# Values projected first, row parts among the first scores, in a fused decoder layer on one core

## The reference, cut to what matters

```python
# x: (2, 256, 512)   ctx: (2, 512, 512)
x = layernorm(x + self_attention(x))      # 32 heads of 16, causal, ALiBi bias, w_attn 512x1536, w_proj 512x512
x = layernorm(x + cross_attention(x, ctx))# 32 query heads, 8 key/value heads of 128, keys from [ctx; x], rms-normed q and k
x = layernorm(x + ffn(x))                 # block-diagonal, permuted
# self_attention:
qkv = x @ w_attn + b_attn; q, k, v = split(qkv, 3)
scores = where(causal, q @ k.T / 16 + slope * (j - i), -inf)
out = softmax(scores) @ v @ w_proj + b_proj
# cross_attention (keys and values):
kv = concat([ctx, x]); k = rms_norm(kv @ Wk) * k_norm; v = kv @ Wv
```

## Time and profile before

| | us |
|---|---|
| median of 3 runs | 844.86 (843.57 to 845.25) |
| profiled execution | 844.77, its span 843.0 |
| PE busy in the span | 826.2 (98%) |
| DVE, ACT, POOL busy | 547.3, 475.4, 522.6 |
| granted clock of TensorE | 0.999 of full |

### The profile page before, as it was taken

The page is one execution under the profiler, slowest core; times in us unless marked ns, Lnnn a source line. Parts: engine busy times, 40 slices in busy tenths (PEclk is TensorE's granted clock), DMA queues, the critical chain, the costliest instruction groups (busy, mean ns, idle before and its releaser), DMA issues.

```text
span 843.0 us, 15129 instructions
## 1 busy us (share of the span) xinstructions
PE 826.2 (98%) x4851; PEld 694.1 (82%) x4851; DVE 547.3 (65%) x1507; ACT 475.4 (56%) x1006; POOL 522.6 (62%) x676
## 2 busy tenths in 40 slices
PE   7999999999999999999999999999999999999997
PEld 5777777777788888888888888888888888888874
DVE  4456566766355677667767676667766766777664
ACT  4666665666246655455555555555545555556554
POOL 3477876757426476766666755775676566636931
PEclk9999999999999999999999999999999999999999
DMA  6613223222141721112102111121122100100101
GB/s 197 199 54 113 75 77 114 63 66 62 51 138 51 243 74 52 50 58 69 51 19 76 34 64 68 37 68 68 37 61 75 38 2 19 63 1 1 26 1 51
DMA packets 48510, 56.22 MB, mean 67 GB/s; under 512 B 4670, under 2 KB 29772, under 8 KB 48460
## 3 DMA queue, kind: packets, MB, share of 16 engines
q1 hardware_dynamic: 48460, 55.59, 21.0%
HBM read 41.95 MB, written 13.63 MB: 66 GB/s over the span
## 4 chain that ended last, share of the span: by engine, by line
PE 62%; DVE 2%; ACT 2%; issue 0%; POOL 0%; POOLq 0%
PE bank L1537 15%; PE bank L48 11%; PE bank L50 11%; PE bank L49 11%; PE bank L1594 9%; PE bank L1527 1%; ACT prob L1351 1%; DVE x_mx L1422 1%; ACT prob L1742 1%; PE bank L1867 0%; PE bank L1868 0%; DVE pT_lo L1471 0%; PE bank L1899 0%; PE bank L1909 0%; PE bank L1908 0%
## 5 line engine op out<-in xcount | busy, mean ns | idle before, releaser
L1253 POOL TENSOR_SCALAR prob<-prob,x_rinv 128x768 f32<-128x768 f32 x124 | 112.9, 911 | 166.8 <-DVE x_rinv L1431 166.8
L1368 ACT ACTIVATE pT_hi<-bank 128x512 fp32r<-128x512 f32 x192 | 114.4, 598 | 90.2 <-PE bank L1594 89.2
L1351 ACT ACTIVATE prob<-bank,x_nm,q_rms 128x768 f32<-128x768 f32 x124 | 123.3, 994 | 47.2 <-DVE x_nm L1425 46.8
L1471 DVE TENSOR_TENSOR pT_lo<-bank,pT_hi 128x512 fp32r<-128x512 f32 x192 | 130.3, 679 | 5.4 <-ACT pT_hi L1368 4.0
L1422 DVE TENSOR_REDUCE x_mx<-bank 128x1 f32<-128x768 f32 x124 | 118.2, 953 | 21.9 <-PE bank L1537 21.6
L1594 PE MATMUL bank<-ident,prob 128*128 128x128 f32 x768 | 115.0, 272 | 2.1 <-POOL prob L1253 1.3
L1594 PEld LDWEIGHTS bank<-ident,prob 128*128 128x128 f32 x768 | 95.0, 140 | 14.2 <-POOL prob L1253 2.0
L48 PE MATMUL bank<-pT_hi,xv_hi 128*128 128x512 f32 x192 | 86.5, 451 | 0.4 <-DVE pT_lo L1471 0.2
L485 ACT ACTIVATE s_self<-s_self,nm_self 128x128 f32<-128x128 f32 (+1 forms) x128 | 57.1, 448 | 43.0 <-DVE nm_self L628 42.4
L50 PE MATMUL bank<-pT_hi,xv_lo 128*128 128x512 f32 x192 | 75.7, 394 | 0.0
L49 PE MATMUL bank<-pT_lo,xv_hi 128*128 128x512 f32 x192 | 75.4, 393 | 0.0
(11 more groups left out here) (234 smaller groups left out, 2048.2 us busy)
## 6 DMA issues: line engine op xcount, KB each, us to landing
wo_raw<-in_Wo SPq DMA_DIRECT2D x8, 1024.0 KB, 5.1
v_by_head<-v_st SPq DMA_DIRECT2D x12, 512.0 KB, 3.6
kT_by_head<-kT_st SPq DMA_DIRECT2D x12, 512.0 KB, 3.2
xk_raw<-kT_by_head SPq DMA_DIRECT2D x16, 384.0 KB, 3.1
xv_raw<-v_by_head SPq DMA_DIRECT2D x16, 384.0 KB, 3.2
wq_raw<-in_Wq SPq DMA_DIRECT2D x6, 1024.0 KB, 5.5
wq_raw<-in_w_attn SPq DMA_DIRECT2D x12, 256.0 KB, 4.1
xk_raw<-in_ctx SPq DMA_DIRECT2D x8, 256.0 KB, 2.6
```

The lines of the kernel that those rows point to most:

```text
L1253: nc.gpsimd.tensor_scalar(prob[:, s, :], prob[:, s, :], rinv[:, s:s + 1], 1.0, ALU.mult, ALU.mult)\
L1351: nc.scalar.activation(prob[:, s, :].rearrange("p (a e) -> p a e", a=2), bank[:, at:at + 2, 0:HALF], ACT.Exp, bias=nm[:, s:s + 1], scale=q ...
L1368: nc.scalar.activation(pT_hi[:, a, :], bank[:, turn.bank[s, what, a], :], ACT.Copy)\
L1471: nc.vector.tensor_tensor(pT_lo[:, a, :], bank[:, turn.bank[s, what, a], :], f32(pT_hi[:, a, :]), ALU.subtract).then_inc(ring_out, 1)
```

## The change

The value weights (group 2 of w_attn) become weight group 0, queries and keys groups 1 and 2. x and the value weights are loaded alternately, piece by piece. PE projects values of a row tile as soon as it and a weight piece are split, then queries, then keys; the context's first tile is transposed between queries and keys, into bank 1; the bias columns go through bank 0. The first four parts stand between S(0) and S(1). The low halves of groups 3 and 5 (Wk's first half, Wv's first) move from POOL to DVE; those of group 6 are placed piece by piece. The cycles that begin with S(3), S(5), S(7) and S(8) lose their last part, so from S(9) on the list has the parts where it had them. As CT(0) has left the ring, banks 4 and 7 change roles.

```diff
-    order = [("S", 0), ("W", 5), ("V", 0), ("E", (0, 0)), ("V", 1), ("E", (0, 1)), ("V", 2), ("E", (0, 2)), ("CT", 0), ("CX", 0), ("V", 3),
-             ("E", (0, 3)), ("R", (0, 0)), ("W", 6), ("R", (0, 1))]
+    order = [("S", 0)]
...
+    order += [("WH6", 0), ("WH6", 1), ("WH6", 2)]
+    parts(1)
+    order.append(("E", (0, 0)))
+    parts(1)
+    order += [("E", (0, 1)), ("WL6", 0), ("WL6", 1)]
+    parts(1)
+    order += [("E", (0, 2)), ("E", (0, 3)), ("R", (0, 0)), ("WL6", 2)]
+    parts(1)
+    order += [("R", (0, 1)), ("WH6", 3), ("WL6", 3)]
...
-        if c < NQ - 1:
+        if c not in (2, 4, 6, 7, NQ - 1):
             parts(1)
...
-        ON_VECTOR, ON_POOL = (0, 1, 2, 4, 6, 8), (3, 5, 7)
+        ON_VECTOR, ON_POOL = (0, 1, 2, 3, 4, 5, 6, 8), (7,)
...
-        before = {4: ("V", 0), 7: ("V", 3), 5: ("V", 1), 6: ("V", 2)}
-        place, quad, rows_over = {}, 0, {}
+        before = {4: ("K", 0), 7: ("K", 3), 5: ("K", 1), 6: ("K", 2)}
+        place, quad, rows_over = {("CT", 0): (1, None)}, 0, {}
...
+                    if p == 0:
+                        sp.dma_start(x[:, i, :], d["x"].rearrange("b s d -> (b s) d")[tokens(i), :]).then_inc(x_in[i], 16)
...
+            load_context(0)
             load_weights(2)
-            load_context(0)
...
+            def values(i, j):
+                pe.wait_ge(xt_lo, j + 1)
+                pe.wait_ge(w_los, i + 1)
+                last = three_passes(nc, bank[:, 4 + j, :], xT_hi[:, i, tokens(j)], xT_lo[:, i, tokens(j)],
+                                    w_hi[:, 0, i, :], w_lo[:, 0, i, :], i == 0, i == KT - 1)
+                if i == KT - 1:
+                    last.then_inc(v_ps, 1)
+
+            row_transposes(0)
+            row_transposes(1)
+            values(0, 0)
+            row_transposes(2)
+            for i, j in ((0, 1), (1, 0), (1, 1)):
+                values(i, j)
+            row_transposes(3)
+            for i, j in ((0, 2), (1, 2), (2, 0), (2, 1), (2, 2), (0, 3), (1, 3), (2, 3)):
+                values(i, j)
+            for j in range(TT):
+                values(KT - 1, j)
+            pe.wait_ge(bias_in, 48)
+            nc.tensor.transpose(bank[:, 0, 0:NCOLS], col_rows[:], ident[0:NCOLS, 0:NCOLS]).then_inc(col_ps, 1)
             for m in range(2 * KT):
+                if m == KT:
+                    context_transposes(0)
+                if m < KT:
+                    pe.wait_ge(v_out, 2 * (m + 1))
...
+                else:
+                    pe.wait_ge(col_out, 1)
+                    pe.wait_ge(ct_lo, 1)
```

More of the change, by code:

```diff
@@ L520, in copy_keys, with take_values_of @@
                 nc.scalar.activation(k_sq[:], k_rows[:, w, :], ACT.Square).then_inc(ksq_made, 1)
+            def take_values_of(j):
+                act.wait_ge(v_ps, j + 1)
+                for odds in range(2):
+                    lanes = slice(odds * SA_DIM, (odds + 1) * SA_DIM)
+                    nc.scalar.activation(padded[odds][:, j, :, lanes],
+                                         bank[:, 4 + j, :].rearrange("p (g e) -> p g e", e=2 * SA_DIM)[:, :, lanes],
+                                         ACT.Copy).then_inc(v_out, 1)
             for j in range(TT):
@@ L525, in _, with queries_of @@
                     .then_inc(xt_hi, 1)
[L526 to L529, removed]
+                weights_hi(0, j)
             for i in range(KT):
                 weights_hi(1, i)
+            act.wait_ge(zeros, 2)
+            for j in range(TT):
+                take_values_of(j)
+            act.wait_ge(col_ps, 1)
+            nc.scalar.activation(cols[:], bank[:, 0, 0:NCOLS], ACT.Copy).then_inc(col_out, 1)
             act.wait_ge(col_out, 1)
-            for m in range(KT):
+            def queries_of(m):
                 act.wait_ge(qk_ps, m + 1)
@@ L536, in _, with keys_of @@
                     .then_inc(q_out, 1)
[L537 to L541, removed]
+            def keys_of(m):
                 act.wait_ge(qk_ps, KT + m + 1)
@@ L544, in _ @@
                                      scale=even[:]).then_inc(k_out, 1)
-                weights_hi(4, m)
-            act.wait_ge(zeros, 2)
-            for what, a in ORDER:
[L548 to L555, removed]
+            for i in range(KT):
+                weights_hi(2, i)
+            queries_of(0)
+            queries_of(1)
+            weights_hi(3, 0)
+            weights_hi(3, 1)
+            queries_of(2)
+            weights_hi(3, 2)
+            weights_hi(3, 3)
+            weights_hi(4, 0)
+            queries_of(3)
+            context_hi(0)
+            for i in range(1, KT):
+                weights_hi(4, i)
+            act.wait_ge(nw_made, 2)
+            keys_of(0)
+            weights_hi(5, 0)
+            weights_hi(5, 1)
+            keys_of(1)
+            weights_hi(5, 2)
+            weights_hi(5, 3)
+            keys_of(2)
+            keys_of(3)
+            for what, a in ORDER:
+                if what == "CX":
                     context_hi(a)
@@ L569, in _ @@
                         weights_hi(a, i)
+                elif what == "WH6":
+                    weights_hi(6, a)
                 elif what == "WH":
@@ L676, in _, with odd_keys @@
                                         f32(xT_hi[:, :, tokens(j)]), ALU.subtract).then_inc(xt_lo, 1)
-            for p in range(2):
-                for i in range(KT):
-                    early_lo(p, i)
+                early_lo(0, j)
+            for i in range(KT):
+                early_lo(1, i)
+            def odd_keys(m):
+                dve.wait_ge(qk_ps, KT + m + 1)
+                dve.wait_ge(k_out, m + 1)
+                nc.vector.tensor_scalar(kT_odd[:, m, :], bank[:, 4 + m, :], cols[:, KT + m:KT + m + 1],
+                                        odd[:], ALU.add, ALU.mult).then_inc(k_odd_out, 1)
+            for i in range(KT):
+                early_lo(2, i)
             dve.wait_ge(col_out, 1)
@@ L685, in _ @@
             for i in range(KT):
[L686 to L692, removed]
+                early_lo(3, i)
+            early_lo(4, 0)
+            context_lo(0)
+            for i in range(1, KT):
+                early_lo(4, i)
+            odd_keys(0)
+            early_lo(5, 0)
+            early_lo(5, 1)
+            odd_keys(1)
+            early_lo(5, 2)
+            early_lo(5, 3)
+            odd_keys(2)
+            odd_keys(3)
             for what, a in ORDER:
@@ L696, in _ @@
                         early_lo(a, i)
+                elif what == "WL6":
+                    early_lo(6, a)
                 elif what == "CX":
@@ L796, in drained, with context_transposes, row_transposes @@
                     pe.wait_ge(vg_late, i[0] + 1)
-            pe.wait_ge(const, 4)
-            for j in range(TT):
+            def context_transposes(n):
+                pe.wait_ge(c_in, 16 * (n + 1))
+                if n > 0:
+                    drained("CT", n)
+                for i in range(KT):
+                    last = nc.tensor.transpose(bank[:, bank_of("CT", n), tokens(i)], c_raw[:, tokens(i)], ident[:])
+                last.then_inc(ct_ps, 1)
+            def row_transposes(j):
                 pe.wait_ge(x_in[j], 16)
@@ L815, in _ @@
                     if m % KT == 0:
-                        pe.wait_ge(w_los, m + i + 1)
-                    last = three_passes(nc, bank[:, 4 + m % KT, :], w_hi[:, m // KT, i, w], w_lo[:, m // KT, i, w],
+                        pe.wait_ge(w_los, KT + m + i + 1)
+                    last = three_passes(nc, bank[:, 4 + m % KT, :], w_hi[:, 1 + m // KT, i, w], w_lo[:, 1 + m // KT, i, w],
                                         xT_hi[:, i, :], xT_lo[:, i, :], i == 0, i == KT - 1)
                 last.then_inc(qk_ps, 1)
[L821 to L828, removed]
             def scores(c):
@@ L870, in weigh_values @@
                 last.then_inc(o_ps, 1)
[L872 to L877, removed]
             def key_transposes(n, g):
@@ L912, in _ @@
             for what, a in ORDER:
[L913 to L915 removed]
+                if what == "S":
                     scores(a)
```

38 lines of the change are left out of this document (14 added, 24 removed).

## The result

| | before | after |
|---|---|---|
| median of 22 runs each, us | 844.78 (842.07 to 845.47) | 846.12 (844.77 to 847.21) |
| ratio to the kernel before, 95% interval | | 1.0022 (1.0016 to 1.0028) |
| profiled execution (span), us | 844.77 (843.0) | 846.42 (844.6) |
| DVE, POOL busy, us | 547.3, 522.6 | 554.2, 513.7 |

Forecast 845.9, measured 846.12. By the medians the kernel is slower by 1.3 us (0.16%); the ratio on record, 1.0022, is not the quotient of the two medians (1.0016). The two lie on either side of what I had called no change (0.2%). Behind the small number stand a gain of 4.2 us and a loss of 5.9 us; the trace shows both. One execution of the kernel before took 1661.77 us beside four of the experiments (split in pieces, attention copy first, E and R ahead, opening alone); it is counted in their median of 844.14 and left out of the ratios.

What follows compares the result with a forecast made beforehand. PE was taken as the bound, hardly ever idle after 10 us. From 844.77: opening -3.2, old waits -1.8, clock +0.45, new waits +5.5, sum +0.95; with the median 0.1 above, 845.9 us, range 842.2 to 848.0.

Steps and rivals of the forecast that it cites:

- S1: Scores of quad 1, which begin the cycle of that name: forecast at 50.6 us, plus 0.45 for the clock.
- the opening's gain: Up to S1, projections start earlier as x and value weights arrive alternately: 3.2 us gained, less 0.45 for the clock.
- The walk through POOL's queue: Queue-by-queue account of what each self-attention cycle waits for after the cut: new waits of 5.5 us in sum.
- S5: Cycle beginning with the scores of quad 5: PE waits 2.0 us, the cycle lasting 11.8 against 9.8 of work.
- S8: Cycle beginning with the scores of quad 8: a key normalisation queued ahead on POOL makes PE wait 1.6 us.
- S7: Cycle beginning with the scores of quad 7: a key quartet waits for PV2's bank, 0.95 us.
- S9: Cycle beginning with the scores of quad 9: a key quartet waits for PV3's bank, 1.0 us.
- W7: Split of w_proj's low half on POOL, 5.0 us, forecast to run from 2.8 to 7.8 us after S5.
- The first: Rival: POOL and DVE keep ahead in S7 to S9, waits of 3.5 us go, 842.4 us; chance 0.27.
- The third: Rival: first matmul not before 9 us because x's second tile lands late, 847.5 us; chance 0.10.
- The second: Rival: the opening's clock rises only at 15.0 us, costing 1.5 us, 847.4 us; chance 0.18.
- The 12.0 for the rise: In the opening, PE's clock was taken to rise at 12.0 us instead of 11.1 at best, 0.45 us lost.

Runs made afterwards that it cites:

- split in pieces: Kernel after, with POOL's block of four w_proj split pieces cut into one piece at the end of each of four cycles: 843.33 us, ratio 0.9987.
- attention copy first: Kernel after, with the copies that set PV's bank free placed ahead of the next exponential in the DVE and ACT lists: 843.54 us, ratio 0.9993.
- E and R ahead: Kernel after, with E(c+1,3) and R(c+1,0) ahead of the part just before T(c,3) in the first eight cycles, PE's order unchanged: 844.35 us, ratio 1.0000.
- opening alone: Kernel after, without the four parts between the first two score groups and with no cycle cut: 847.93 us, ratio 1.0044.
- kernel before with two edits: Kernel before, with w_proj's last split one piece a cycle and the attention copies ahead of the next exponential: 842.39 us, ratio 0.9983.
- all three edits: Kernel after, with w_proj's split one piece a cycle, attention copies ahead of the exponential, and E and R ahead of the last part: 840.49 us, ratio 0.9955.
- opening alone, filled: Kernel after without the early parts or cut cycles, plus sixteen identity matmuls on PE ahead of the second score group: 845.38 us, ratio 1.0014.

## Why the prediction was right

**By its steps.** First matmul 6.91 (forecast 6.85). S1 at 51.37 (51.05): 0.3 of the opening's gain was missing. PE has no wait from there to S0, and the rise came where I had it; the 0.3 is in changes of kind, which I had taken at nothing. Where the kind of work changes, the next start is later: 0.57 instead of 0.43 at the lower clock (9.04 to 9.61), and 0.34 instead of 0.23 at the full one (21.73 to 22.07). Five such steps between the rise and S0 make 0.46; from S0 to S1 it took 0.14 less than my sum. The edits "at nothing" (low halves to DVE, value copies first, SP's queue, new waits in the opening) cost nothing that a wait shows.

**The cycles.** The walk through POOL's queue held at each of its stations. Timeline of POOL in the kernel after, answering to the earlier trace rows:

```profile
94.55 5.04 POOL L417 TENSOR_TENSOR wq_lo<-wq_raw,wq_hi 128x512 fp32r<-128x512 f32 x4
99.58 0.36 POOL L430 TENSOR_SCALAR s_self<-s_self,rinv_self 128x128 f32<-128x128 f32 x1
...
126.71 0.37 POOL L430 TENSOR_SCALAR s_self<-s_self,rinv_self 128x128 f32<-128x128 f32 x1
```

The last split ends 7.8 after S5 (99.59) as forecast, and R(7,0) starts 1.5 after S8 (126.71), behind the key normalisation. The lost time, each beside an experiment that took it away:

| cycle | forecast wait | with | without, and by which edit | wait |
|---|---|---|---|---|
| S5 | 2.0 | 11.80 | 9.81, split in pieces | 2.0 |
| S6 | 0 | 10.44 | 10.15, split in pieces, but see there | 0.3 |
| S7 | 0.95 | 11.19 | 10.26, attention copy first | 0.9 |
| S8 | 1.6 | 9.96 | 8.39, E and R ahead of the part | 1.6 |
| S9 | 1.0 | 12.26 | 11.20, attention copy first | 1.1 |

Sum 5.9, forecast 5.5. Missed was S6, taken at nothing: E(6,3) is 0.18 late for S7 (114.00). That this is what is left of W7's delay is likely and not shown. With 0.3 for the opening, 0.3 for S6, 0.1 for S9 and the rounding, the forecast's +0.95 becomes the measured 1.67 at S10. By the medians the difference is 1.34, and the miss 0.4.

**The rivals.** The first (helpers keep ahead in S7 to S9) is refuted: 3.6 us of waits stand there, and each goes by the edit that its cause asks for (S9's comes back when S8's alone is taken away). The third is refuted by 6.91. The second put the clock's rise at 15.0; it came at 12.2, 5.3 after the first matmul, and between 8.9 and 11.7 in the six other profiles with the same opening (table below). That is also against the other time that I had weighed: by the Trainium skill (TensorE: Matmul & The Clock Gate, Part 4) transposes don't count as busy for the clock gate, from which I had worked out 14.2; the four transposes at 8.33 to 9.04 held up no rise in any of these profiles. The run with ten extra ones could not tell what transposes do by themselves, but another profile can: in that of the kernel before with two edits, the sixteen row transposes from 3.55 to 6.86 are all that PE has done, and the last of them run at the full level.

```profile
L800 PE MATMUL bank<-ident,x_rows x16: 272/417/444, 3.6 to 6.6; 128*128 128x128 f32 x16
```

The durations (shortest, median, longest, ns) are those of both levels: 417 at the lower one (no transpose of x in the kernel before took less) and 272 at the full one. So transposes alone can bring the rise. Where the page and this trace differ, the trace decides; my reading in the prediction, that the transposes from 3.60 brought none, was right for its one profile and no rule.

**What was luck.** The 12.0 for the rise was a single draw. The profiles with the same opening, by the start from which matmuls are 0.24 us apart:

| kernel | rise, us | S0, us |
|---|---|---|
| after | 12.2 | 44.84 |
| all three edits | 11.7 | 44.54 |
| attention copy first | 10.9 | 44.29 |
| split in pieces | 10.4 | 43.99 |
| opening alone | 10.3 | 43.90 |
| E and R ahead of the part | 10.0 | 43.77 |
| opening alone, filled | 8.9 | 43.25 |

S0 moves by half of what the rise moves (1.6 for 3.3), as the prediction had it, but the profile after happens to be the latest of seven. The Trainium skill (TensorE: Matmul & The Clock Gate, Part 1) says that the moment of the rise differs from run to run, with where in the gate's own cycle the first work falls, and gives 0.5 us either way; the traces agree that it differs, but by 3.3 us from the earliest to the latest. The kernel before draws too: with two edits far behind this stretch its S1 stood 1.7 us earlier than in the earlier trace rows, from which the opening's gain is reckoned. So that the sum came out within 0.2 us is in part luck; a single profile of this kernel can't be forecast more closely than these draws allow.

**Still open.** Whether plain matmuls bring the rise sooner than transposes is not shown: the clock was full early with ten and with five plain ones, with sixteen row transposes in one profile, and not with ten extra transposes, one profile each. The medians with ten extra transposes (1.0010) and without (1.0022) differ by about what the chance of the clock gives in one profile, and their intervals meet. The opening alone with the clock held is 0.6 us ahead of before in the profiles and behind it in the medians (1.0005 to 1.0023); each profile is one draw. With all three edits S6 lasts 10.48, 0.33 above its work, and the trace names no wait in it; 0.25 of it lies ahead of the T at 109.91.

## What to carry to other kernels

When work is moved from a late cycle to an early one, the engine in front gains at once and the helpers' lists stay as they were: write out, for each shortened cycle, what stands in each helper's list ahead of the release that the front engine waits for, since the work taken out was their cover. Then move the release forward in that list (split the long block, put the copy that frees a bank first), and look at all such places together, because a wait cleared in one cycle can come back in the next (E and R ahead of the part did that, the two other edits did not). Fill a long idle time of TensorE with real work, or with matmuls that delay nothing: here 4.34 us of idle time cost another 2.4 by the clock.

## What was not expected of the hardware

- 4.34 us of idle time on TensorE took the granted clock from 1.00 to 0.50 (the lower level, 1.2 GHz) until 54.5 us, 5.3 us after work had begun again, worth 2.4 us of the 11.76 us cycle.
- The rise at the start of one and the same opening moved from 8.9 to 12.2 us between profiles. Timeline of PE in the kernel before with two edits far behind this stretch; the clock was at the full level at 9.04, behind 2.18 us of idle time, fell at 9.84 and rose again at 13.24, within one unbroken row of matmuls:

```profile
9.04 0.47 PE L48 MATMUL bank<-x_hi,w_hi 128*128 128x512 f32 x1 [2.18 <-DVE w_lo L615]
...
9.84 0.63 PE L48 MATMUL bank<-x_hi,w_hi 128*128 128x512 f32 x1
...
12.82 0.58 PE L49 MATMUL bank<-x_lo,w_hi 128*128 128x512 f32 x1
13.24 0.39 PE L50 MATMUL bank<-x_hi,w_lo 128*128 128x512 f32 x1
```

- In the same profile only f32 row transposes had run when the clock rose for the first time; in the kernel before, sixteen of them with a gap of 0.29 us brought no rise.
- With five plain f32 matmuls of 128 by 128 where PE waits for x (drawn with 1.65 and 1.06 us), the full clock was there at the first projection matmul (6.82), and S10 came 2.0 us earlier than with the three edits alone. With ten it was there by 7.30. Without them it was never there before 8.9 in seven profiles of this opening. They are drawn as two records each.
- The granted clock that the profile gives for the opening is no help: it reads 1.00 from 10 to 15 us in the kernel before, where starts are 0.43 apart. The level there is read from starts and durations; in the profile above, where the clock had risen once, it reads 0.50 from 10 to 13.
